# Two layer norms' variance from squares on ScalarE, a gate factor in one-column steps, and new orders on every engine of a transformer layer

## The reference, cut to what matters

```python
def layernorm(x): return (x - mean(x)) / sqrt(var(x) + 1e-5)

x = x + layernorm(attention(layernorm(x)))     # x: 32 batches x 256 rows x 128; 16 heads of 64
x = x + layernorm(ffn(layernorm(x)))

def ffn(x):                                    # 8 experts of rank 16
    gate = softmax(x @ gate_w.T)
    t    = einsum('nh,erh->ner', x, lora_U)
    return x @ weight.T + einsum('ne,eor,ner->no', gate, lora_V, t) / 16
```

## Time and profile before

| | us |
|---|---|
| median of 3 runs (lowest to highest) | 1117.65 (1117.55 to 1120.37) |
| the profiled execution, and its span from first to last instruction | 1118.4, 1116.6 |
| busy in the span: TensorE, VectorE | 1018.4 (91%), 1022.7 (92%) |
| busy: ScalarE, GpSimd | 833.8 (75%), 678.0 (61%) |

### The profile page before, as it was taken

The page is one execution under the profiler, slowest core; times in us unless marked ns, Lnnn a source line. Parts: engine busy times, 40 slices in busy tenths (PEclk is TensorE's granted clock), DMA queues, the critical chain, the costliest instruction groups (busy, mean ns, idle before and its releaser), DMA issues.

```text
span 1116.6 us, 28105 instructions
## 1 busy us (share of the span) xinstructions
PE 1018.4 (91%) x8550; PEld 774.4 (69%) x8550; DVE 1022.7 (92%) x2075; ACT 833.8 (75%) x2855; POOL 678.0 (61%) x682
## 2 busy tenths in 40 slices
PE   8889899999999999999999999999999999999965
PEld 7667677677677777677767667767767777767743
DVE  7899899999999999999999999999999999999962
ACT  5778777778777777877777877777877777787741
POOL 2565666565666665666665566656566666566541
PEclk9899999999999999999999999999999999999996
DMA  6555566555556655556655556655555655555660
GB/s 234 122 123 115 114 140 155 123 117 132 117 132 155 136 116 132 116 120 155 148 116 121 127 117 146 155 122 116 133 116 134 155 134 116 133 115 122 155 161 10
DMA packets 59222, 145.26 MB, mean 130 GB/s; under 512 B 17216, under 2 KB 25920, under 8 KB 59200
## 3 DMA queue, kind: packets, MB, share of 16 engines
q1 hardware_dynamic: 59200, 144.99, 56.2%
HBM read 6.50 MB, written 4.19 MB: 10 GB/s over the span
## 4 chain that ended last, share of the span: by engine, by line
POOL 42%; issue 30%; DVE 11%; PE 8%; SPq 4%; ACT 1%; POOLq 1%; DMA 1%; DVEq 0%; ACTq 0%
POOL probs L1502 32%; SPq L269 4%; POOL rstd L1482 4%; DVE neg_max L1079 4%; PE o_ps L435 3%; DVE qk_lo L1074 2%; DVE probs_b L1095 2%; POOL xn L1491 2%; POOL xn L1496 1%; POOL z L1509 1%; POOL var_eps L1475 1%; DVE stats L1003 1%; PE st_ps L413 1%; DMA probs_t<-probs_b 1%; DVE mean_var L1008 1%
## 5 line engine op out<-in xcount | busy, mean ns | idle before, releaser
L1502 POOL TENSOR_TENSOR probs<-probs,inv_sum 128x1024 f32<-128x1024 f32 x256 | 484.3, 1897 | 321.9 <-DVE inv_sum L1087 321.9
L727 ACT ACTIVATE probs<-st_ps,neg_max 128x256 f32<-128x256 f32 x1024 | 477.8, 485 | 26.3 <-DVE neg_max L1079 25.3
L1079 DVE TENSOR_REDUCE neg_max<-st_ps 128x4 f32<-128x1024 f32 x256 | 309.9, 1210 | 4.4 <-PE st_ps L413 4.0
L1095 DVE STREAM_TRANSPOSE probs_b<-probs 128x1024 f32<-128x1024 f32 x256 | 312.8, 1222 | 0.8 <-POOL probs L1502 0.8
L435 PE MATMUL o_ps<-probs_t,v_sb 128*64 128x256 f32 x2048 | 254.8, 391 | 15.6 <-DMA probs_t<-probs_b 14.7
L727 ACT ACTIVATION_READ_ACCUMULATOR probs<-st_ps,neg_max 128x1 f32 x1024 | 221.2, 216 | 0.0
L435 PEld LDWEIGHTS o_ps<-probs_t,v_sb 128*64 128x64 f32 x2048 | 138.0, 138 | 105.1 <-issue 17.8
L720 ACT CAST qk_hi<-qk_ps 128x512 fp32r<-128x512 f32 x256 | 152.5, 596 | 46.4 <-PE qk_ps L381 46.1
L413 PE MATMUL st_ps<-qk_hi 64*128 64x256 f32 x1024 | 171.7, 330 | 8.7 <-ACT probs L727 7.7
L1074 DVE TENSOR_TENSOR qk_lo<-qk_ps,qk_hi 128x512 fp32r<-128x512 f32 x256 | 170.5, 667 | 2.5 <-ACT qk_hi L720 2.2
L413 PEld LDWEIGHTS st_ps<-qk_hi 64*128 64x128 f32 x1024 | 98.0, 185 | 69.5 <-issue 44.8
(11 more groups left out here) (130 smaller groups left out, 1837.6 us busy)
## 6 DMA issues: line engine op xcount, KB each, us to landing
probs_t<-probs_b SPq DMA_DIRECT2D x1024, 128.0 KB, 2.3
out<-x_all SPq DMA_DIRECT2D x31, 128.0 KB, 2.0
x_all<-in_x SPq DMA_DIRECT2D x1, 3840.0 KB, 17.6
probs_b<-in_w_v SPq DMA_DIRECT2D x1, 512.0 KB, 4.9
probs_b<-in_w_o SPq DMA_DIRECT2D x1, 512.0 KB, 6.8
probs_b<-in_w_q SPq DMA_DIRECT2D x1, 384.0 KB, 5.4
probs_b<-in_w_k SPq DMA_DIRECT2D x1, 384.0 KB, 6.0
x_all<-in_x SPq DMA_DIRECT2D x2, 128.0 KB, 3.4
```

The costliest lines, as they stand in the source:

```text
L727: last = nc.scalar.activation(probs[n][:, h, j, :], st_ps[p % 2][:, (2 * h + j) * T:(2 * h + j + 1) * T], ACT.Exp, bias=neg_max[n][:, h, j ...
L1079: nc.vector.tensor_reduce(neg_max[p % N_PROBS][:, :, :].rearrange("p h j -> p (h j)"), st_ps[p % 2][:, :].rearrange("p (j s) -> p j s", j= ...
L1095: nc.vector.transpose(probs_b[chunk % 2][:, :, :, 2 * NT * n:2 * NT * (n + 1), :].rearrange("p i t n q -> p n t i q"), probs[p % N_PROBS][ ...
L1502: nc.gpsimd.tensor_tensor(probs[n][:, :, :, :].rearrange("p h j s -> p (h j) s"), probs[n][:, :, :, :].rearrange("p h j s -> p (h j) s"), ...
```

## The change

LN_Y and LN_Z no longer go through VectorE: ScalarE squares the two tiles in PSUM, scaled so that its accumulator output is the mean square, which is the variance of zero-mean rows (`square_y`, `square_z`). `copy_z` stays, behind the squares, and `norm_z` now waits for it. For LN_X and LN_X1 the statistics are two calls, `spread_...` and `aggregate_...`, with other work between them, and the carrying copy is gone from the loop. The gate factor is two `tensor_scalar` of one column, called apart from `gate_max`. And the calls stand in a new order on all engines; TensorE's loop begins one batch earlier, and `project_z` is done in the same turn of the loop as the rest of its batch.

```diff
-        stats = [sb(f"stats{n}", [P, NT, 6]) for n in range(4)]
+        stats = [sb(f"stats{n}", [P, NT, 6]) for n in range(2)]
         stats_seen = sb("stats_seen", [P, 1])
-        mean_var = [sb(f"mean_var{n}", [P, NT, 2]) for n in range(4)]
+        mean_var = [sb(f"mean_var{n}", [P, NT, 2]) for n in range(2)]
+        mean_square = [sb(f"mean_square{n}", [P, NT]) for n in range(2)]
+        squares = [sb(f"squares{n}", [P, NT * D]) for n in range(2)]
...
-        LN_X, LN_Y, LN_X1, LN_Z = range(4)
+        LN_X, LN_X1, LN_Y, LN_Z = range(4)
+        variance = [mean_var[0][:, :, 1], mean_var[1][:, :, 1], mean_square[0][:, :], mean_square[1][:, :]]
+        ROOT_MEAN = D ** -0.5
...
             def body(i):
                 transpose_xn(i, free=(v_copied[3], i))
-                scores(i - 1, 7)
                 project_qk(i, 0)
-                project_z(i - 3, free=(xt_lo_ready, i + 1))
                 project_qk(i, 1)
-                output_projection(i - 2, free=(z_copied, i - 2))
+                output_projection(i - 2, free=(xt_lo_ready, i + 1))
+                project_qk(i, 2)
+                transpose_y(i - 2, free=(yt_ready, i - 1))
                 scores(i, 0)
-                project_qk(i, 2)
+                scores(i, 1)
                 project_qk(i, 3)
-                transpose_y(i - 2, free=(yt_ready, i - 1))
-                scores(i, 1)
                 probs_v(i - 1, 0)
                 probs_v(i - 1, 1)
+                scores(i, 2)
                 project_qk(i, 4)
-                scores(i, 2)
-                project_qk(i, 5)
                 project_v(i, 0, free=(x1_ready, i - 1))
                 probs_v(i - 1, 2)
                 probs_v(i - 1, 3)
                 scores(i, 3)
+                project_qk(i, 5)
+                transpose_x1(i - 2, free=(v_copied[0], i + 1))
+                scores(i, 4)
+                project_tg(i - 2, free=(x1t_ready, i - 1))
                 project_qk(i, 6)
-                transpose_x1(i - 2, free=(v_copied[0], i + 1))
                 project_qk(i, 7)
-                project_tg(i - 2, free=(x1t_ready, i - 1))
-                scores(i, 4)
+                scores(i, 5)
                 probs_v(i - 1, 4)
+                transpose_u(i - 2, free=(u_ready, i - 1))
                 probs_v(i - 1, 5)
-                scores(i, 5)
-                transpose_u(i - 2, free=(u_ready, i - 1))
                 project_v(i, 1, free=(ut_ready, i - 1))
+                scores(i, 6)
+                project_z(i - 2, free=(v_copied[1], i + 1))
                 probs_v(i - 1, 6)
                 probs_v(i - 1, 7)
-                project_v(i, 2, free=(v_copied[1], i + 1))
-                scores(i, 6)
+                project_v(i, 2, free=(z_copied, i - 1))
+                scores(i, 7)
                 project_v(i, 3, free=(v_copied[2], i + 1))
...
+            def mean_squares(ln, ps):
+                for j in range(NT):
+                    last = nc.scalar.activation(tile(squares[ln - LN_Y], j), ps[j], ACT.Square, scale=ROOT_MEAN,
+                                                accum_out=mean_square[ln - LN_Y][:, j:j + 1])
+                last.then_inc(variance_ready[ln], 1)
+            def square_y(b):
+                act.wait_ge(y_transposed, b + 1)
+                mean_squares(LN_Y, [tile(extra_ps, j) for j in range(NT)])
+            def square_z(b):
+                act.wait_ge(z_projected, b + 1)
+                after(act, rstd_ready[LN_Z], b)
+                mean_squares(LN_Z, [tile(extra_ps, j) for j in range(NT)])
+            def square_last_z():
+                act.wait_ge(z_projected, B - 1 + NT)
+                act.wait_ge(rstd_ready[LN_Z], B - 1)
+                mean_squares(LN_Z, last_z_ps)
...
-            def ln_stats(ln, src, count):
+            def spread(ln, src):
                 for j in range(NT):
                     last = nc.vector.bn_stats(stats[ln][:, j, :], tile(src, j))
                 last.then_inc(stats_ready[ln], 1)
-                dve.wait_ge(stats_ready[ln], count)
-                nc.vector.tensor_copy(stats_seen[:, :], stats[ln][:, NT - 1, 0:1])
+            def spread_landed(ln, b):
+                dve.wait_ge(stats_ready[ln], b + 1)
+                if ln == LN_X:
+                    after(dve, xn_ready, b)
+            def aggregate(ln):
                 for j in range(NT):
                     last = nc.vector.bn_aggr(mean_var[ln][:, j, :], stats[ln][:, j, :])
-                last.then_inc(mean_var_ready[ln], 1)
+                last.then_inc(variance_ready[ln], 1)
+            def settle():
+                nc.vector.tensor_copy(stats_seen[:, :], one[:, :])
...
-            def stats_x(b):
+            def spread_x(b):
                 dve.wait_ge(x_loaded[min(b, 2) if isinstance(b, int) else 2], 16)
-                after(dve, xn_ready, b)
-                ln_stats(LN_X, x_tiles(b), b + 1)
+                after(dve, variance_ready[LN_X], b)
+                spread(LN_X, x_tiles(b))
+            def aggregate_x(b):
+                aggregate(LN_X)
...
-            def stats_y(b):
-                dve.wait_ge(y_transposed, b + 1)
-                ln_stats(LN_Y, extra_ps, b + 1)
...
+            def spread_x1(b):
                 dve.wait_ge(x1_ready, b + 1)
-                ln_stats(LN_X1, x1, b + 1)
+                after(dve, variance_ready[LN_X1], b)
+                spread(LN_X1, x1)
+            def aggregate_x1(b):
+                aggregate(LN_X1)
...
+            def scale_gate_max(b):
+                dve.wait_ge(gate_max_found, b + 1)
                 dve.wait_ge(rstd_ready[LN_X1], b + 1)
-                dve.wait_ge(gate_max_found, b + 1)
-                nc.vector.tensor_tensor(gate_neg_max[:, :], gate_max_raw[:, :], rstd[LN_X1][:, :],
-                                        ALU.mult).then_inc(gate_max_ready, 1)
+                for j in range(NT):
+                    last = nc.vector.tensor_scalar(gate_neg_max[:, j:j + 1], gate_max_raw[:, j:j + 1],
+                                                   rstd[LN_X1][:, j:j + 1], None, ALU.mult)
+                last.then_inc(gate_max_ready, 1)
...
-            def stats_z(b):
-                dve.wait_ge(z_copied, b + 1)
-                ln_stats(LN_Z, z, b + 1)
...
             def norm_z(b):
+                pool.wait_ge(z_copied, b + 1)
                 pool.wait_ge(rstd_ready[LN_Z], b + 1)
```

More of the change, by code:

```diff
@@ L867, in _ @@
-            gate_exponentials(0)
-            exponentials(2, 3, 1)
+            exponentials(2, 4, 1)
             attention_hi(1, 2)
-            qk_hi(2, 6)
             copy_ut(0)
             exponentials(2, 4, 0)
-            exponentials(2, 4, 1)
             copy_v(2, 1)
+            qk_hi(2, 7)
             exponentials(2, 5, 0)
+            square_z(0)
+            copy_z(0)
+            exponentials(2, 5, 1)
             copy_v(2, 2)
+            exponentials(2, 6, 1)
+            copy_v(2, 3)
@@ L877, in _ @@
             attention_hi(1, 3)
-            qk_hi(2, 7)
-            copy_v(2, 3)
-            exponentials(2, 5, 1)
-            xt_high(3)
-            exponentials(2, 6, 0)
-            exponentials(2, 6, 1)
-            copy_z(0)
-            qk_hi(3, 0)
-            qk_hi(3, 1)
-            exponentials(2, 7, 0)
-            exponentials(2, 7, 1)
-            copy_yt(1)
-            exponentials(3, 0, 0)
-            qk_hi(3, 2)
-            qk_hi(3, 3)
-            exponentials(3, 0, 1)
-            attention_hi(2, 0)
@@ L1254, in _ @@
+            invert_sum(1, 5)
+            row_max(1, 6)
+            spread_landed(LN_X, 2)
+            qk_lo(1, 7)
+            aggregate_x(2)
             transpose_blocks(1, 4)
+            row_max(1, 7)
+            spread_x(3)
+            invert_sum(1, 6)
             xt_low(2)
             attention_lo(0, 3)
-            row_max(1, 7)
-            invert_sum(1, 6)
+            transpose_blocks(1, 5)
+            spread_landed(LN_X, 3)
+            invert_sum(1, 7)
+            aggregate_x(3)
@@ L1273, in _ @@
             row_max(2, 2)
-            stats_x1(0)
+            qk_lo(2, 3)
+            spread_landed(LN_X, 4)
+            invert_sum(2, 1)
+            aggregate_x(4)
+            spread_landed(LN_X1, 0)
+            transpose_blocks(2, 0)
+            aggregate_x1(0)
             qk_lo(2, 4)
-            transpose_blocks(2, 0)
             row_max(2, 3)
             attention_lo(1, 1)
+            qk_lo(2, 5)
             gate_max(0)
-            invert_sum(2, 1)
+            invert_sum(2, 2)
@@ L1295, in _ @@
             qk_lo(2, 7)
             row_max(2, 6)
-            xt_low(3)
+            transpose_blocks(2, 4)
             invert_sum(2, 5)
-            transpose_blocks(2, 4)
-            row_max(2, 7)
-            invert_sum(2, 6)
-            stats_z(0)
-            transpose_blocks(2, 5)
-            qk_lo(3, 0)
-            transpose_blocks(2, 6)
-            invert_sum(2, 7)
-            qk_lo(3, 1)
-            row_max(3, 0)
-            stats_y(1)
```

(64 more changed lines are left out.)

619 lines of the change are left out of this document (266 added, 353 removed).

## The result

The changed kernel takes 1143.18 us (median of 4, 1142.65 to 1143.47), where the kernel before took 1117.6 beside it: ratio 1.0231, 95% interval 1.0200 to 1.0262. It is slower by 25.6 us; the forecast was 15 us faster. The profiled execution took 1143.47 us.

A forecast was written before the change was run, and what follows sets the result against it. TensorE and VectorE were nearly level; relieved, VectorE would no longer bind. TensorE's period would be 30.35 + 2.2 + 0.15 + 0.05 = 32.75 us; 1118.4 - 11.5 - 3.7 = 1103.2, median 0.75 lower: 1102.4, range 1093 to 1114.

The forecast's parts named there:

- 33.16 - 2.8 = 30.35 us of TensorE work that the change doesn't touch: TensorE's loop: old period of 33.16 us less 2.8 lost to waits leaves 30.35 of fixed work a batch.
- 0.9 + 1.31 us lost in one place: TensorE's batch boundary: 0.9 us lost ahead of transpose_xn and 1.31 between it and project_qk, 2.2 instead of 1.4.
- (b): Rival on TensorE's loop: old waits stay behind other causes, boundary's +0.8 is paid, nothing given back; 1136 us, chance 0.06.
- VectorE's relief: VectorE, a batch: 0.73 + 0.73 + 0.3 + 0.64 = 2.4 us less, from statistics, the carrying copy and the gate.
- Rival (e): Gate on VectorE: one-column steps are held by GpSimd, 1 us a batch, period 33.6 and 1125 us; chance 0.03.
- The squares: ScalarE: 0.37 us a square, 0.75 a pair, 1.5 a batch, hidden behind TensorE's scores and probs_v.
- The way of 1.68 us: Boundary: from the start of the transposes to project_qk, through three engines, 1.68 us that the change doesn't shorten.
- The boundary's loss: TensorE between batches: 2.2 us lost instead of 1.4 with project_qk directly behind transpose_xn, +0.8 a batch.
- two tenths of small waits: TensorE inside the batch: 0.15 us at project_tg, 0.05 altogether at scores of pair 2 and project_z.
- The three old waits: TensorE inside the batch: waits for x1 (0.5 us), exponentials (0.4) and u's copy (0.55) go, 1.45 in all.
- Beginning and end: Outside the loop: beginning 0, within 3 us; end -3.7, from transfers starting 2.2 earlier and a last chain 1.5 shorter.
- The working's 28 batches: TensorE's new loop: 0.41 us less a batch over 28 batches, 11.5 us in all.

The follow-up runs named there:

- e1_fill: The changed kernel with 8 added matmuls of 128x256, results unused, between transpose_xn and the first project_qk: 1099.5 us, ratio 0.985.
- e11_fill_ahead: The changed kernel with 6 added matmuls of 128x256, results unused, ahead of transpose_xn and none behind it: 1100.21 us, ratio 0.9837.
- e3_bare: The kernel before with the scores call between transpose_xn and the first project_qk moved ahead of the last project_v: 1180.74 us, ratio 1.0579.
- e2_split: The changed kernel with the scores call ahead of the last project_v put back between transpose_xn and the first project_qk: 1112.0 us, ratio 0.995.
- e8_best: e2_split with the last probs_v moved between project_v 2 and 3, and copy_z ahead of the squares of z, which read the copy: 1140.33 us, ratio 1.0198.
- e10_fill3: The changed kernel with 3 added matmuls of 128x256, results unused, between transpose_xn and project_qk: 1137.82 us, ratio 1.0177.
- e6_gate_tt: The changed kernel with the gate's factor made by one tensor_tensor of two columns again: 1142.84 us, ratio 1.0215.

## Why the prediction was wrong

**The bound and the period.** The step that failed is "33.16 - 2.8 = 30.35 us of TensorE work that the change doesn't touch". It took the length of the work as fixed. The change touches it through the clock: the two waits of the boundary now stand with nothing but 0.37 us of transposes between them, the granted clock falls to 1.2 GHz for about 3.4 us, and the work in it takes 1.5 us longer (32.65 against 34.17). The working had every piece, 0.9 + 1.31 us lost in one place, and asked only what that waiting costs. It doesn't mention the clock: the 1.00 of the earlier trace rows was carried over in silence, though it belonged to the order of the calls. None of the rivals had the clock; (b) came out nearest in time, by another mechanism.

The Trainium skill, "TensorE: Matmul & The Clock Gate", section "Part 1: The HAM clock gate (the "warmup" mystery)", says that the throttled level is the default and activity releases it, and its section "HAM oscillation — how this bites in real kernels" tells of a kernel that falls back in every tile. The trace agrees: once a batch, and an addition of work brought 43.7 us. The same section charges throttled time at half, by which 3.4 us would cost 1.7, an estimate; measured 1.5. Some 0.2 us of the 3.4 lie in the wait ahead of `project_qk` (517.56).

**VectorE's relief.** 57.5 us on the page is 1.8 a batch of busy time, against 2.4 with the short waits counted. The gate's steps have 210 ns each and leave VectorE after 0.25 together (forecast 0.16), in their timeline from 503.19 to the next instruction at 503.44. Rival (e) is out: none of 128 steps in two traces took over 218 ns. But what relief is worth depends on the orders: in before's the gate's part brought 8 to 9 us by itself and nothing together with the squares (1118.83), and in the new ones it brought nothing (1142.84).

**The squares.** Forecast 0.37 each, 0.75 a pair. Measured in the timeline of ScalarE, 0.52 for a pair:

```profile
510.60 0.28 ACT L725 ACTIVATE squares<-extra_ps 128x128 f32<-128x128 f32 x1
...
510.87 0.27 ACT L725 ACTIVATE squares<-extra_ps 128x128 f32<-128x128 f32 x1
...
511.12 0.37 ACT L765 COPY z<-extra_ps 128x256 f32<-128x256 f32 x1
```

That they are hidden where they stand was right: the changed kernel's list of waits has none of TensorE for what stands behind them.

**The new order.** Right in the terms that the waits decide, and to 0.1 us in their sum. The way of 1.68 us: 1.68. The boundary's loss and two tenths of small waits: period 32.75 with the clock up, measured 32.66 in e1_fill and 32.67 in e11_fill_ahead, where the small waits don't appear. The three old waits gone: gone.

**Beginning and end.** From `xt_high` of batch 31 to the end of the span it was 81.97 us before and is 78.95 in the changed kernel (1141.6 - 1062.65), 78.6 in e1_fill: -3.0 and -3.4 for the forecast -3.7. The transfers start 27.45 us behind that `xt_high` in e1_fill, forecast 27.7; in the changed kernel 28.91, since the batch has its slow stretch in it:

```profile
1091.56 20.89 SPq L273 DMA_DIRECT2D probs_t<-probs_b  x32
```

**The sum.** 1102.4 was forecast for a clock at its upper level; with that restored it is 1099.5. The clock's 1.5 us in each of 27 periods are 41 of the 43.7 us between that and 1143.2; the rest lies ahead of them: `xt_high` of batch 4 starts at 137.69 in e1_fill, 2.35 earlier. The working's 28 batches are one too few: TensorE's new loop has 29 turns (e1_fill has 8782 - 8550 = 232 instructions more, 8 a turn), which is worth 0.4 us.

**Left open.** Why equal boundaries lower the clock in every batch of the changed kernel, in one of three in e3_bare and in 10 of 27 in e2_split. No run varied that alone, and how many batches of e2_split and e3_bare have a fall was counted in one execution of each.

## What to carry to other kernels

Waits of TensorE have a price beyond their length: before an order puts two of them side by side, look at TensorE's busy share and the granted clock in windows of one microsecond, before and after, and keep some work between them. Where TensorE's busy time grows with an unchanged count of instructions, look at the clock first; cheap dummy matmuls in the idle stretch are a quick test, and can be the remedy (1143.2 to 1099.5). Relief of an engine pays only where the orders use it: name which wait of the bounding engine it ends, and check what is then queued behind the moved work.

## What the runs showed of the hardware

- Waits of 0.76 and 1.25 us, with 0.37 us of transposes between, sufficed for the granted clock to fall to 0.50. With 6 matmuls (0.7 us) in the first wait or 8 (0.95) in the second it never fell; with 3 in the second it fell in 24 of 27 batches.
- A fall lasts about 3.4 us in each of four traces (the changed kernel, e2_split, e3_bare, e8_best). It costs 1.5 us where TensorE is packed behind it (e10_fill3) and 0.9 in e2_split and e3_bare; in e2_split waits that stood behind it swallow a part.
- Equal waits at a boundary don't always have the same effect on the clock (e3_bare: 9 of 27).
- VectorE's `tensor_tensor` of two columns beside GpSimd took 160 ns at the least and 867 in the median of 32 (in e6_gate_tt's orders 366); `tensor_scalar` of one column took 203 to 218 in each of 128.
